# Two expert loads into x's halves, logits copied ahead of the norms, routing numbers placed sooner, and the first two steps of each attention turned by TensorE

## What is computed

```python
x = x + _L0_xattn_ref(_layernorm(x, axis=-1), ctx_1024, ...)   # scores, softmax over 8192, values, out projection
x = x + _L0_attn_ref(_layernorm(x, axis=-1), ...)
...
xz = xn @ in_w.T + in_b
x_proj, z = (xz[..., :D_MODEL], xz[..., D_MODEL:])
z = jax.nn.silu(z)
y = _ssm_scan(x_proj, A_log, B_param, C_param, log_dt)   # rfft of length 2L, product, irfft
y = y * z
y = y @ out_w.T + out_b
return jnp.clip(y + residual, -10.0, 10.0)
...
x = x + _L0_ffn_ref(_layernorm(x, axis=-1), ...)
...
logits = xt @ gate_w + gate_b
sel = jnp.argmax(softmax(logits), axis=-1)
y_all = jnp.einsum('td,edh->eth', xt, expert_w) + expert_b[:, None, :]
out = jnp.einsum('te,eth->th', onehot(sel), y_all)
```

## Time and profile before

| | us |
|---|---|
| median of 3 runs (1149.94 to 1151.09) | 1150.84 |
| the profiled execution | 1147.02 |
| its span | 1145.3 |
| PE busy in the span | 1094.6 |
| PE busy in the 24.0 us from 1066 to 1090 | 12.09 |

### The profile page before, as it was taken

One profiled execution on the slowest core, in us unless ns is written; L12 is line 12 of the kernel. 1 busy time (PEld: TensorE's weight loads), 2 busy tenths in 40 slices (PEclk: granted clock), 3 DMA queues, 4 the chain that ended last, 5 costly groups with the idle time before them and its releaser, 6 DMA issues.

```text
span 1145.3 us, 16465 instructions
## 1 busy us (share of the span) xinstructions
PE 1094.6 (96%) x4945; PEld 883.5 (77%) x4945; DVE 847.7 (74%) x1768; ACT 524.3 (46%) x1108; POOL 535.7 (47%) x588
## 2 busy tenths in 40 slices
PE   7999999999999999999999999999999999987498
PEld 5787867788888888878878888888888888874375
DVE  7963597898888888777277777777776656898494
ACT  4221165565555555442464444444444352545261
POOL 4801254445444444412186576566666531265343
PEclk9999999999999999999999999999999999998689
DMA  8221478968777767423257677677666621026791
GB/s 289 86 72 37 74 191 210 209 187 194 202 175 203 181 186 191 139 85 103 43 152 207 187 188 203 177 200 188 191 179 185 192 85 37 1 90 208 273 383 58
DMA packets 202231, 184.36 MB, mean 161 GB/s; under 512 B 18193, under 2 KB 147249, under 8 KB 202179
## 3 DMA queue, kind: packets, MB, share of 16 engines
q1 hardware_dynamic: 180962, 141.26, 47.5%
q10 hardware_dynamic: 17856, 32.51, 8.1%
q0 software_dynamic: 3360, 9.97, 2.4%
HBM read 142.77 MB, written 42.73 MB: 162 GB/s over the span
## 4 chain that ended last, share of the span: by engine, by line
PE 77%; DVE 11%; issue 4%; DMA 3%; POOL 2%; ACT 1%; SPq 1%; POOLq 0%; ACTq 0%; DVEq 0%
PE bank L631 37%; PE bank L770 28%; PE bank L1019 3%; PE bank L819 3%; PE bank L639 1%; DMA zT<-in_L_ffn_expert_w_dram 1%; DMA resid<-p_rows 1%; DVE h L1479 1%; DMA spectra<-in_ctx_dram 1%; POOL hl_B L1987 1%; DVE bnst L1457 1%; POOL hl_F L1980 1%; PE bank L1005 1%; PE bank L665 1%; DVE probs L365 1%
## 5 line engine op out<-in xcount | busy, mean ns | idle before, releaser
L1164 ACT ACTIVATE probs<-bank,nbias 128x512 f32<-128x512 f32 x128 | 88.1, 689 | 243.8 <-DVE nbias L1602 243.7
L770 PE MATMUL bank<-hl_A,probsT 128*128 128x512 f32 x768 | 190.6, 397 | 2.3 <-issue 2.0
L770 PE MATMUL bank<-hl_F,probsT 128*128 128x512 f32 x768 | 190.4, 397 | 1.9 <-issue 1.7
L631 PE MATMUL bank<-hl_B,hl_D 128*128 128x512 f32 x768 | 185.0, 391 | 4.1 <-POOL hl_B L1987 3.5
L1597 DVE TENSOR_REDUCE mx<-bank 128x1 f32<-128x512 f32 x128 | 87.8, 686 | 133.7 <-PE bank L631 133.5
L631 PE MATMUL bank<-hl_C,hl_D 128*128 128x512 f32 x768 | 185.2, 390 | 0.0
L770 PEld LDWEIGHTS bank<-hl_A,probsT 128*128 128x128 f32 x768 | 144.1, 188 | 37.1 <-issue 2.4
L631 PEld LDWEIGHTS bank<-hl_B,hl_D 128*128 128x128 f32 x768 | 143.8, 188 | 37.1 <-issue 5.0
L770 PEld LDWEIGHTS bank<-hl_F,probsT 128*128 128x128 f32 x768 | 144.1, 188 | 36.6 <-issue 2.1
L631 PEld LDWEIGHTS bank<-hl_C,hl_D 128*128 128x128 f32 x768 | 144.2, 188 | 31.5
L1980 POOL TENSOR_TENSOR hl_F<-stage,hl_F 128x512 fp32r<-128x512 f32 x64 | 84.3, 1317 | 166.4 <-ACT hl_F L1131 166.3
(11 more groups left out here) (412 smaller groups left out, 1856.2 us busy)
## 6 DMA issues: line engine op xcount, KB each, us to landing
p_rows<-probs ACTq DMA_DIRECT2D x124, 256.0 KB, 3.1
stage<-in_ctx_dram SPq DMA_DIRECT2D x112, 256.0 KB, 3.2
spectra<-in_ctx_dram SPq DMA_DIRECT2D x64, 256.0 KB, 6.0
xb<-in_ctx_dram SPq DMA_DIRECT2D x64, 256.0 KB, 5.8
resid<-p_rows SPq DMA_DIRECT2D x248, 64.0 KB, 2.1
h<-p_rows SPq DMA_DIRECT2D x124, 64.0 KB, 2.4
obB<-p_rows SPq DMA_DIRECT2D x124, 64.0 KB, 2.0
stage<-in_L_ffn_expert_w_dram SPq DMA_DIRECT2D x6, 1024.0 KB, 7.5
```

Source lines behind the costliest of these rows:

```text
L631: last = nc.tensor.matmul(dst, lhs[:, a, t, k * P:(k + 1) * P], rhs[:, c, t, :], start=(t == 0 and (a, c) == PASSES[0]), stop=(t == T - 1 ...
L770: last = nc.tensor.matmul(obank[u % 2][:], probsT[u % 2][:, a, j, :], nat[b][par][:, c, j, :], start=(j == 0 and (a, c) == PASSES[0]), sto ...
L1164: nc.scalar.activation(dst, src, ACT.Exp, bias=nbias[:, q:q + 1], scale=SCALE, accum_out=rsum[:, q:q + 1]).then_inc(probs_ready, 1)
```

## The change

First: the first two steps of each attention are turned by PE too (`FIRST` = 2), behind the scores of steps 1 and 2; `put_probs`, `move_probs` and `turn_moved` are left out for them. Second: W6 and W7 go into x's halves in place of zT and rows, and wait for x's stores and the normalized rows rather than for the rows' stores and a gather; W5 is issued ahead of x's second store; the chosen experts' buffers move round. Third: ACT rounds W3 ahead of the first copy of turned rows, copies both batches' logits ahead of both norms, and rounds weights one loop step later, behind the turned rows; the second batch's logits are made in two parts of 256 rows. Fourth: on DVE the low halves of the normalized rows stand ahead of a gate addition, and the first group of the second output half ahead of the low halves of the first. Fifth: POOL's routing numbers are computed at the end of the second attention, its masks where both stood.

```diff
-RAW = (0, 4, 5, 0, 1, 0, 2, 3, 6, 7, 1, 0, 2, 3, 6)
+RAW = (0, 4, 5, 0, 1, 0, 6, 7, 2, 3, 1, 0, 6, 7, 2)
...
-MOVED = STEPS - 2
+FIRST = 2
+MOVED = STEPS - FIRST - 2
...
+for _k in range(2):
+    EVACUATED.remove(f"yT.{_k}@0")
+    EVACUATED.insert(EVACUATED.index("u.0@1"), f"yT.{_k}@0")
...
-                    if n < MOVED:
-                        move_probs(b, n)
+                    if FIRST <= n < FIRST + MOVED:
+                        move_probs(b, n - FIRST)
...
+                    elif n in (6, 7):
+                        sp.wait_ge(x_stored, 16 * B)
+                        sp.wait_ge(ffn_rows, T * (n - 5))
                     else:
                         sp.wait_ge(norm_stored, 16 * B * 2)
-                        sp.wait_ge(x_stored, 16 * B)
...
             fixed_load(4)
             store_x(0)
             fixed_load(3)
+            fixed_load(5)
             store_x(1)
             for b in range(B):
                 for half in range(2):
                     store_rows(b, half)
-            fixed_load(5)
-            sp.wait_ge(gathered[2], 16)
             fixed_load(6)
             fixed_load(7)
             sp.wait_ge(experts_chosen, 1)
+            sp.wait_ge(gathered[2], 16)
             for g in range(E, GROUPS):
                 chosen_load(g)
 
...
                     for u in range(UN):
                         scores(t, u)
+                        if first and 0 < u <= FIRST:
+                            if u == 1:
+                                for job in last_on_tbank[b]:
+                                    evacuated_from(job)
+                            turn_probs(t, u - 1)
...
-                gate_logits(0)
+                gate_logits(0, 1)
                 for t in range(2, T):
                     turn_ffn(1, t)
-                gate_logits(1)
+                gate_logits(1, 2)
...
+            def gate_logits(b, parts):
                 dst = open_bank(f"logits@{b}")
-                evacuated_from(f"ffnT.3@{b}")
-                for k in range(T):
-                    last = nc.tensor.matmul(dst[0:E, :], gate_raw[:, k, :], spectra[:, T * b:T * b + T, k * P:(k + 1) * P],
-                                            start=(k == 0), stop=(k == T - 1))
+                n = T // parts
+                for m in range(parts):
+                    evacuated_from(f"ffnT.{n * m + n - 1}@{b}")
+                    for k in range(T):
+                        last = nc.tensor.matmul(dst[0:E, n * m * P:n * (m + 1) * P], gate_raw[:, k, :],
+                                                spectra[:, T * b + n * m:T * b + n * (m + 1), k * P:(k + 1) * P],
+                                                start=(k == 0), stop=(k == T - 1))
                 last.then_inc(filled, 1)
...
-                def exponentials(t, u, for_pe=False):
+                def exponentials(t, u, first, for_pe):
                     q = u % T
-                    wait_pos(act, p_put[u % 2], 16 * (MOVED // 2) * b, t * (16 * UN // 2) + 16 * (u // 2))
+                    if first and FIRST <= u < 2 * FIRST:
+                        act.wait_ge(pT_ready, (FIRST + 2) * b + u - FIRST + 1)
+                    wait_pos(act, p_put[u % 2], 16 * (MOVED // 2) * b, t * (16 * UN // 2) + 16 * ((u - FIRST) // 2))
...
                         if not (first and u < LAG - 1):
-                            turned_probs(*back(t, u, LAG - 1))
-                        exponentials(t, u, last and u >= UN - 2)
-                        if not (last and u >= UN - 2):
+                            turned_probs(*back(t, u, LAG - 1), first and u < LAG - 1 + FIRST)
+                        for_pe = first and u < FIRST or last and u >= UN - 2
+                        exponentials(t, u, first, for_pe)
+                        if not for_pe:
                             put_probs(t, u)
                         natural(t, u, first)
                         if kernel_terms:
...
                 weights(2)
+                weights(3)
                 turned_ffn(0, range(T))
                 turned_ffn(1, range(2))
-                weights(3)
                 copy_logits(0)
                 turned_ffn(1, range(2, T))
-                normalize_outputs(0)
                 copy_logits(1)
-                normalize_outputs(1)
+                for b in range(B):
+                    normalize_outputs(b)
                 weights(4)
                 turned_tokens(0)
                 turned_tokens(1)
                 weights(5)
                 for g in range(GROUPS):
-                    if g + SLOTS < GROUPS:
-                        weights(g + SLOTS)
                     if g + 2 < GROUPS:
                         turned_tokens(g + 2)
+                    if 0 < g and g + SLOTS - 1 < GROUPS:
+                        weights(g + SLOTS - 1)
 
             prepare()
             attention(0, True)
...
-                            turned_probs(*back(t, u, LAG - 1))
-                        if not (first and u < 2):
+                            turned_probs(*back(t, u, LAG - 1), first and u < LAG - 1 + FIRST)
+                        if not (first and u < 2 + FIRST):
...
-            def outputs(c):
-
-                dve.wait_ge(copied, COPIED[f"U0i.{c}@1"])
-                output_products(dve, nc.vector, 0, TRIPS + c, c * S, S, wide_parts)
-                dve.wait_ge(copied, COPIED[f"U1i.{c}@1"])
-                for group in range(1, 5):
+            def outputs(c, groups):
+
+                if 0 in groups:
+                    dve.wait_ge(copied, COPIED[f"U0i.{c}@1"])
+                else:
+                    dve.wait_ge(copied, COPIED[f"U1i.{c}@1"])
+                for group in groups:
                     output_products(dve, nc.vector, group, TRIPS + c, c * S, S, wide_parts)
 
             def outputs_lo(c):
...
+                lo_rows("normT.#@1", hlA)
                 gate_output(0, range(2))
-                lo_rows("normT.#@1", hlA)
                 inputs_in_place()
-                outputs(0)
+                dve.wait_ge(iota_made, 1)
+                outputs(0, range(1))
+                outputs(0, range(1, 5))
+                outputs(1, range(1))
                 outputs_lo(0)
                 gate_output(0, range(2, T))
-                outputs(1)
+                outputs(1, range(1, 5))
                 outputs_lo(1)
...
-                    if g + 2 + EARLY < GROUPS:
-                        weight_los(g + 2 + EARLY)
+                    if 0 < g and g + SLOTS - 1 < GROUPS:
+                        weight_los(g + SLOTS - 1)
...
-            def routing_tables():
-
-                counts = obB[:, 0:P].bitcast(I32)
-                filled_by(pool, "U1i.1@1")
-                pool.wait_ge(product_step, PRODUCTS * (TRIPS + 2))
+            def routing_numbers():
+
+                counts = probs[1][:, 0:P].bitcast(I32)
+                filled_by(pool, "inT0.3@1")
                 chain(nc.gpsimd.iota(counts, [[1, P]], base=0, channel_multiplier=0))
...
+            def routing_masks():
+
+                filled_by(pool, "U1i.1@1")
+                pool.wait_ge(product_step, PRODUCTS * (TRIPS + 2))
...
                 outputs_lo()
+                routing_numbers()
                 add_out_bias(0)
                 gated_lo()
-                routing_tables()
+                routing_masks()
                 add_out_bias(1)
                 for g in range(EARLY):
```

13 lines of the change are left out of this document (7 added, 6 removed).

## The result

The changed kernel takes 1136.61 us (median of 4 runs, 1135.32 to 1140.49) against 1150.96 before (median of 4): a ratio of 0.9881, 95% interval 0.9856 to 0.9907. That is 14.35 us less by the medians (13.7 by the ratio), where 9.9 were forecast.

What follows compares the result with a forecast made beforehand. PE bounds the kernel (busy 96%), with savings only where it waits; -1.2 - 0.5 - 0.8 + 0.5 - 7.9 = -9.9 us off the median 1150.84 gives 1140.9, own range 1138.5 to 1144, 8-in-10 range 1136 to 1146.5.

Steps and rivals of the forecast that it cites:

- The two loads: Group loop: W6 and W7 issued sooner end PE's idle and the low clock behind it, -7.9 us.
- Rival B: Group loop: the wait moves from W6 to the next load or the gathers, about 1146 us; chance 0.15.
- The first attention: First weighing 0.85 us earlier and 0.35 of a later 2.44 wait gone: -1.2, between -3.3 and +1.2.
- case A: More returned: both attention waits go and W3's rounding holds the copies half as long, 1136.3 us; chance 0.15.
- The second attention: First weighing there, behind an idle of 1.66 us: -0.5, between -1.7 and +1.2.
- DVE's list: Convolution: low halves first (1.1) and an output group filling DVE's wait (1.39), rounded to -2.3 us; range -1.2 to -3.6.
- The logits: Around the logits: turned +0.9 us later, +1.7 for a low clock, -1.1 for a wait gone ahead of the ranks.
- +0.5 for the first gather: Group loop's start: W6 and W7 load while the first gathers run, +0.5 us, range 0 to +2.7.
- The carrying to the medians: Whole kernel: the 9.9 us taken off the profiled 1147.02 also comes off the median of 1150.84, giving 1140.9.

Runs made afterwards that it cites:

- the repeated run: The changed kernel run once more with no edit: 1135.52 us, ratio 0.9879 to the kernel before.
- the loads alone: The kernel before with only W6 and W7 loaded into x's halves, behind the rows' stores, and the experts' buffers moved round: 1142.56 us, ratio 0.9938 to before.
- the order alone: The kernel before with only the group loop's order changed, turned rows first and weights behind them: 1147.15 us, ratio 0.9974 to before.
- turns undone: The changed kernel with the first two steps of each attention turned through DRAM again: 1142.13 us, ratio 0.9945 to the kernel before.
- norm between: The changed kernel with the first norm back between ACT's copies of the two batches' logits: ratio 0.9865 to the kernel before.
- W3 back: The changed kernel with ACT's rounding of W3 back behind the six copies of turned rows: 1134.08 us, ratio 0.9862 to the kernel before.
- the low halves back: The changed kernel with the normalized rows' low halves back behind the gate addition on DVE: ratio 0.9879 to the kernel before.
- loads late: The changed kernel with W6 and W7 issued behind the wait for the third gather again, still into x's halves: 1139.44 us, ratio 0.9919 to before.
- the group back: The changed kernel with the first group of the second output half back behind the first half's low halves: ratio 0.9885 to the kernel before.
- numbers back: The changed kernel with POOL's routing operations back behind its low halves in the convolution, without DVE's wait for them: ratio 0.9881 to the kernel before.

## Why the prediction was right, and where its sizes were off

The direction, the range (1136.0 to 1146.5) and the main term held: 1136.61 lies inside, but only 0.6 above the low end, and the repeated run's 1135.52 would lie outside: more came back than the forecast of 1140.9 has, and that the range held is in part luck. Point by point:

- **The two loads, -7.9.** -7.83 between the second and fourth mix in the traces, and 7.1 timed for the loads alone. Right in size. The prediction gave it to the loads alone; the reordering in the group loop, for which it has no term, removes the same wait too, though alone it is worth only 3.0. With both in, undoing the loads costs a wait of 1.1 in the trace and about 4 by the times, where alone they are worth 7. Rival B (the wait goes to a later load or the gathers) didn't occur with the loads early. With them late, and with the order alone, later loads were late.
- **The first attention, -1.2, with ends at -3.3 and +1.2.** This step failed: from the product ahead of it to 498.59 before, and to 496.68 after, are 366.06 and 362.02, a gain of 4.0, beyond the end of the range. Two terms were mis-sized. A turn was priced at its record's length of 0.60, while PE's next product starts 0.39 and 0.35 behind a turn's start: 0.74 in all, not 1.2. And the prediction took only 0.35 of the 2.44 wait as gone. The waits in this attention were 2.05, 2.44 and the smaller ones below that it left out, 6.4 together, and are 2.2 in after (0.60, 0.63 and 0.97). Before, in the timeline:

```profile
143.91 5.72 PE L631 MATMUL bank<-hl_B,hl_D 128*128 128x512 f32 x24 [0.22 <-DVE obB L1557]
149.96 5.87 PE L631 MATMUL bank<-hl_B,hl_D 128*128 128x512 f32 x24 [0.33 <-ACT probs L1164]
...
163.18 0.97 PE L770 MATMUL bank<-hl_A,probsT 128*128 128x512 f32 x3 [0.24 <-POOL hl_A L1980]
...
228.90 3.03 PE L631 MATMUL bank<-hl_B,hl_D 128*128 128x512 f32 x12 [1.09 <-POOL hl_B L1987]
```

  The path to the 2.44 was misread too. The prediction has the context block's load late in SP's list. In the trace of before ACT had rounded that block's last part by 172.79, but POOL's work on it stood behind a piece of the next values, and this behind ACT, which was held by a put that waited for an earlier step's move:

```profile
179.80 0.63 ACT L1131 ACTIVATE hl_F<-stage 128x512 fp32r<-128x512 f32 x1 [4.89 <-DMA resid<-p_rows]
...
181.80 1.25 POOL L1987 TENSOR_TENSOR hl_B<-spectra,hl_B 128x512 fp32r<-128x512 f32 x1
```

  ACT's wait is 4.30 with the turns undone and 2.68 in after. So a move's landing was the cause, as the prediction says, but through two engines' lists and not through a load. That much returned was in case A, at 0.15; it deserved more.
- **The second attention, -0.5.** 1.66 became 0.41 at the price of 0.74: -0.5. By position it is 0.3 (89.79 us between the two attentions' rows at 498.59 and 588.38, and 89.52 after). Right within that.
- **DVE's list, -2.3.** The low halves gave 1.2 (forecast 1.1) and the group in the wait 1.6 (forecast 1.39). Of the contention the prediction booked neither gain nor loss, and for DVE the trace bears that out: three L372 operations take 1.67 to 1.78 while POOL lowers the gated rows, and before there were three slow L365 operations too (not the four that the prediction has as its most), only that it is other operations now. POOL's side of it the prediction left out: the stretch has grown from 6.73 to 11.84 us. One of POOL's four took 6.05, while eight L372 operations ran one behind the other beside it at 0.69 each:

```profile
992.22 11.84 POOL L2139 TENSOR_TENSOR hl_F<-zT,hl_F 128x512 fp32r<-128x512 f32 x4 [27.39 <-ACT hl_F L1284]
...
995.83 0.69 DVE L372 TENSOR_TENSOR probs<-resid,spectra 128x512 f32<-128x512 f32 x1
```

  The first of the eight began at 994.62, POOL's long one within 0.1 behind it. So POOL paid 5 us here besides DVE's 3.2. The Trainium skill's page "SBUF — State Buffer" ("Who interferes with whom") says that the order of issue, and not the operation, decides who is blocked, and this trace agrees. POOL's end at 1004.06 stands just ahead of the block that PE begins at 1004.16 after an idle 0.82, and PE's later wait of 1.31 for DVE covers that.
- **The logits.** Forecast: 3.9 later copies, half-speed logits for 1.7, a clock regained for 1.1, net +1.5 on the route. Measured from 5.0 ahead (1038.91 to 1033.89, the turned rows) to 3.4 ahead at the first gather: +1.6. The parts differed. W3 landed in 7.2, so the copies were 2.8 late on the route, and the first logits took 6.52, so the clock cost 2.9. The prediction took the removed norm to be what freed the logits' copy, and the run with the norm between shows that it isn't: with the late logits the norm fits in ACT's wait. With W3 back, the wait ahead of the first logits and its low clock vanish.
- **+0.5 for the first gather**: 7.73 us from the slots' product to the first turned rows (1063.48 to 1071.21), 8.21 after (1060.03 to 1068.24). Right. Not in the sum: the first mix took 5.46 rather than 4.14, with more of it at the low clock, +1.3, and the second gather's wait fell from 1.50 to 0.87, -0.6.
- **The carrying to the medians.** The profile of before had started 1 to 3 us early by chance. The sum is made of differences within it and didn't suffer, but the spans of two single executions differ by 10.1 where the kernels differ by 14.

So of the 4.4 us beyond the forecast some 2.9 are the attentions (4.6 against 1.7) and 0.5 DVE's list. The remaining 1 is within the scatter of the logits' clock (the two traces of the same program gain 12.2 and 14.0), and isn't assigned.

## What to carry to other kernels

At the start of a pipelined loop look at every wait of the first steps, not only at the one ahead of the first consumer: here a put that waited for an earlier transfer held the rounding and lowering of later inputs behind it, in the lists of two engines. When an engine waits for a load with other work behind it, both the load's issue and the order in its list can be changed; measure each alone, since together they hide each other's worth. And before a wait is moved ahead of a chain (W3 ahead of the copies here), ask what it holds: in the traces that edit made the logits 4 us later and the fourth mix 1.1 to 3.8, by the times it cost some 2 us, and the gain of the others covered it.

## What the runs showed of the hardware

**The length of a wait of 3 to 4 us didn't settle the clock behind it.** The eight products for the first logits came behind a wait of PE, and took 3.59 at full clock. In the traces:

| kernel | wait, us | the eight products, us |
|---|---|---|
| after | 2.94 | 6.52 |
| the low halves back | 3.63 | 6.33 |
| loads late | 3.81 | 6.44 |
| turns undone | 3.65 | 5.29 |
| norm between | 3.47 | 5.03 |
| the group back | 3.20 | 3.59 |
| the same kernel again | 3.69 | 3.59 |
| numbers back | 1.91 | 3.59 |

Windows of after and of the repeated run in these products:

```profile
1040.00:1045.00 5.00, 5.00 (x7) 0.83 (x6) 4.45 (x21) 0.45 (x1) 1.00 (x1) 0.50 0.43 118
```

```profile
1042.00:1045.00 3.00, 3.00 (x8) 0.54 (x6) 2.66 (x11) 0.70 (x2) 1.25 (x2) 1.00 0.07 21
```

The same program had 1.2 GHz for them in one execution and 2.4 in the other. A wait of 3 to 4 us ahead of 3.6 us of work cost between 0 and 2.9 more here, and a forecast has to hold both. Elsewhere the price was steady: in the convolution a wait of 2.87 or 2.88 stands in four traces (before, loads alone, order alone, the group back), and the eight transforms behind it took 7.34 each time, where they take 5.86 at full clock.

**PE's records overlap by 0.14 to 0.16 at a block's end** (in the rows of the first attention 12 products of 2.98 start at 151.51 and the next block at 154.33; the profile models the ends of products), so a block followed directly costs less than its length, and a removed wait is worth some 0.15 more than it says. For four transposes, recorded at 0.60, that made the price 0.37.
